# An adaLN feed-forward with threshold routing: x loads first, 17 key levels, layer 1's high parts ahead

## The reference, cut to what matters

```
probs = softmax(rotate(x) @ gate_w.T)                    # N x 8
order = argsort(-probs); csum = cumsum(p_sorted)
select_prefix = experts up to the first with csum >= 0.9
R = p_sorted - rank   (rank 1..8; -1e9 where not selected)
topC = the 512 tokens with the largest R, for each expert
scores = probs where selected and in topC, else 0
y = sum over e of scores[:, e] * (gelu(rotate(x) @ w1[e].T) @ w2[e].T)
out = x + y
```

## Time and profile before

| | us |
|---|---|
| median of three runs | 267.33 |
| the profiled execution's own time | 266.72 |
| its span, first to last instruction | 264.9 |
| TensorE busy with matmuls | 243.7 |
| VectorE busy | 199.4 |
| ACT busy | 149.8 |
| POOL busy | 137.0 |

### The profile page before, as it was taken

The page is one execution under the profiler, slowest core; times in us unless marked ns, Lnnn a source line. Parts: engine busy times, 40 slices in busy tenths (PEclk is TensorE's granted clock), DMA queues, the critical chain, the costliest instruction groups (busy, mean ns, idle before and its releaser), DMA issues.

```text
span 264.9 us, 4043 instructions
## 1 busy us (share of the span) xinstructions
PE 243.7 (92%) x1450; PEld 185.0 (70%) x1450; DVE 199.4 (75%) x430; ACT 149.8 (57%) x275; POOL 137.0 (52%) x105
## 2 busy tenths in 40 slices
PE   7788878798998999999999999999999999999970
PEld 2455433245996888888888888888888888888750
DVE  5288889998989967978996798789779966933220
ACT  6431048864566658746765774687467658734100
POOL 1000000037703987887778749766875771487530
PEclk9999999999999999999999999999999999999997
DMA  6999999407798597579658855973994690372521
GB/s 214 422 424 428 503 343 387 149 21 196 261 317 282 195 344 132 161 179 273 166 82 249 241 111 118 294 192 48 219 249 130 85 222 12 42 85 37 182 91 40
DMA packets 12787, 53.81 MB, mean 203 GB/s; under 512 B 2768, under 2 KB 3152, under 8 KB 9552
## 3 DMA queue, kind: packets, MB, share of 16 engines
q1 hardware_dynamic: 4512, 35.72, 37.2%
q0 software_dynamic: 8256, 17.85, 31.8%
HBM read 44.78 MB, written 18.22 MB: 238 GB/s over the span
## 4 chain that ended last, share of the span: by engine, by line
PE 68%; DVE 16%; DMA 8%; issue 2%; POOL 1%; ACT 1%; SPq 0%; POOLq 0%; DVEq 0%
PE bank L828 21%; PE bank L830 20%; PE bank L829 20%; DMA region<-in_xt 7%; DVE region L691 4%; PE bank L810 4%; DVE w1rot L509 3%; DMA xg<-in_x,gath 1%; PE bank L888 1%; POOL xg L298 1%; DVE hl L538 1%; DVE thr L708 1%; DVE xg L637 0%; DVE xg L633 0%; DVE csum L638 0%
## 5 line engine op out<-in xcount | busy, mean ns | idle before, releaser
L314 POOL DMA_INDIRECT out<-ysb,scat x32 | 61.3, 1916 | 34.8 <-ACT ysb L391 22.2
L509 DVE SCALAR_TENSOR_TENSOR w1rot<-w1raw,rot,w1rot 128x512 f32<-128x512 f32 x84 | 63.1, 751 | 5.3 <-ACT w1rot L351 3.4
L298 POOL DMA_INDIRECT xg<-in_x,gath x16 | 19.8, 1235 | 70.5 <-DVE gath L560 56.3
L828 PE MATMUL bank<-xh,w1h 128*128 128x512 f32 (+1 forms) x144 | 53.2, 370 | 0.1
L830 PE MATMUL bank<-xh,w1l 128*128 128x512 f32 (+1 forms) x144 | 52.7, 366 | 0.0
L829 PE MATMUL bank<-xl,w1h 128*128 128x512 f32 (+1 forms) x144 | 52.7, 366 | 0.0
L828 PE MATMUL bank<-w2h,hh 128*128 128x512 f32 x128 | 51.6, 403 | 0.0
L830 PE MATMUL bank<-w2h,hl 128*128 128x512 f32 x128 | 50.0, 390 | 0.0
L829 PE MATMUL bank<-w2l,hh 128*128 128x512 f32 x128 | 49.9, 390 | 0.0
L538 DVE TENSOR_TENSOR hl<-hf,hh 128x512 fp32r<-128x512 f32 x32 | 22.1, 689 | 28.3 <-ACT hh L382 28.3
L378 ACT ACTIVATE hf<-bank 128x512 f32<-128x512 f32 x32 | 19.1, 597 | 36.1 <-PE bank L830 36.1
(11 more groups left out here) (134 smaller groups left out, 332.7 us busy)
## 6 DMA issues: line engine op xcount, KB each, us to landing
region<-in_xt SPq DMA_DIRECT2D x8, 1024.0 KB, 9.4
w1raw<-in_w SPq DMA_DIRECT2D x8, 1024.0 KB, 12.0
w2raw<-in_w SPq DMA_DIRECT2D x8, 1024.0 KB, 8.6
score<-probs_scratch,pidx POOLq DMA_INDIRECT x32, 5.1
out<-ysb,scat POOLq DMA_INDIRECT x32, 6.0
probs_scratch<-probs SPq DMA_DIRECT2D x1, 384.0 KB, 21.1
ch<-in_ch SPq DMA_DIRECT2D x1, 320.5 KB, 10.2
xg<-in_x,gath POOLq DMA_INDIRECT x16, 4.0
```

Of the source, the lines that this page charges most:

```text
L298: pool.indirect_dma_start(xg[e % 2][:, s, :], None, x_d, bass.IndirectOffsetOnAxis(gath[:, e, s:s + 1], 0)).then_inc(xg_in[e % 2][s], 16)
L314: pool.indirect_dma_start(out_d, bass.IndirectOffsetOnAxis(scat[:, e, s:s + 1], 0), ysb[:, s, :], None, compute_op=ALU.add if e < LAST els ...
L509: ins = nc.vector.scalar_tensor_tensor(dst, w1raw[:, e % 2, i, :], rot[:, j, i:i + 1], dst, ALU.mult, ALU.add)
L828: nc.tensor.matmul(dst, ah, bh, start=first, stop=False)
```

## The change

- SP no longer issues `small` and `cf`; ACT does, as its first two instructions, on its own queue. x blocks 0 and 1 are then SP's first.
- There are 17 levels in place of 23. Above 1.25 the intervals are 0.25 wide, below it 0.125. `scale` (minus 1 or minus 2, by `top`) multiplies the keys, so that the search runs on one width; it is one new instruction of VectorE ahead of the keys and two new ones in round 0. The last two steps of the search use it.
- `gath` is written from the first sum directly, without the minimum; x in HBM has 128 more rows of zeros, which a list that is short can point at. `tabf` is computed after it.
- The first `count_tokens` reads the thresholds from PSUM, and the copy to `tb` comes after its scan.
- `layer1` and `layer1_half` issue high x high and low x high for all four chunks of x, and then the four products with `xl`. They wait for `xh` first and for `xl` later.
- For expert 0, `layer2` tile 1 comes ahead of the second pair of transposes.
- 12 filler matmuls at the start in place of 13.

```
@@ -55,21 +55,18 @@
 THRESHOLD = 0.9
-KEY_ULP = 2.0 ** -24
+KEY_ULP = 2.0 ** -23
 ABOVE = 2.0 ** -24 * (1 + 2.0 ** -20)
...
 G8, G9 = 2.0 ** -8, 2.0 ** -9
-WIDTH = 0.125
+WIDTH, WIDTH1 = 0.25, 0.125
 BINS = ([(0.0, 0.0 - G9)] + [(31 * k * G8, 31 * k * G8 - G9) for k in range(1, 8)]
-        + [(1.25, 1.5 - G9)] + [(k * G8, k * G8 - G9) for k in (415, 446, 477)]
-        + [(2.25, 682 * G8)] + [(k * G8, k * G8 - G9) for k in (714, 745)]
-        + [(3.375, 3.75 - G9), (991 * G8, 991 * G8 - G9)]
-        + [(4.375, 1228 * G8), (1259 * G8, 1258 * G8)]
-        + [(5.375, 1493 * G8), (1524 * G8, 1523 * G8)]
-        + [(6.375, 1755 * G8), (7.375, 2015 * G8), (8.5, 8.5 - WIDTH)])
+        + [(1.25, 1.5 - G9), (447 * G8, 447 * G8 - G9), (2.25, 682 * G8), (745 * G8, 745 * G8 - G9), (3.375, 3.75 - G9),
+           (4.375, 1228 * G8), (5.375, 1493 * G8), (6.375, 1755 * G8), (7.375, 2015 * G8), (8.5, 8.5 - WIDTH)])
 TL = len(BINS) - 1
+SPLIT = 1.25
 NL = TL * E
@@ -83,7 +80,7 @@
 CG, NCG = table(("sel", E), ("slot", S4), ("start", KT), ("need", KT), ("step", ROUNDS * KT), ("offset", ROUNDS * KT),
-                ("last", 1), ("tops", NL))
+                ("tops", NL))
 CA, NCA = table(("same", P), ("ones", P), ("levels", NL))
@@ -154,6 +151,7 @@
         edge = sb("edge", [P, 2])
+        scale = sb("scale", [P, 3])
         tb = sb("tb", [P, E])
@@ -240,8 +238,6 @@
         def _(sp):
-            sp.dma_start(small[:, :], small_d).then_inc(small_in, 16)
-
             def load_x(g):
@@ -259,7 +255,6 @@
-            sp.dma_start(cf[:, :], cf_d).then_inc(cf_in, 16)
             load_x(0)
@@ -340,6 +335,8 @@
         def _(act):
+            act.dma_start(small[:, :], small_d).then_inc(small_in, 16)
+            act.dma_start(cf[:, :], cf_d).then_inc(cf_in, 16)
             act.wait_ge(squares, 1)
@@ -556,20 +553,20 @@
                 then(nc.vector.tensor_reduce(tabg[:, :], before_slot[:, :, :], AX.X, ALU.add))
+                nc.vector.tensor_tensor(gath[:, e, :], tabg[:, :], vbank[:, :, NT], ALU.add).then_inc(gath_ready, 1)
                 then(nc.vector.tensor_tensor(tabf[:, :], tabg[:, :], vbank[:, :, NT], ALU.add))
-                nc.vector.tensor_scalar(gath[:, e, :], tabf[:, :], float(N - 1), None, ALU.min).then_inc(gath_ready, 1)
                 then(nc.vector.tensor_scalar(tabg[:, :], tabf[:, :], float(N - 1), None, ALU.min))
...
-            def count_tokens(e0, e1):
+            def count_tokens(e0, e1, edges=tb):
...
                     ins = nc.vector.tensor_tensor(mask[:, e0:e1, m, :], key[:, :, e0:e1].rearrange("p t e -> p e t"),
-                                                  tb[:, e0:e1].unsqueeze(2).to_broadcast([P, w, NT]), op)
+                                                  edges[:, e0:e1].unsqueeze(2).to_broadcast([P, w, NT]), op)
                 then(ins)
@@ -678,7 +675,8 @@
             dve.wait_ge(key_mm, 1)
-            nc.vector.tensor_scalar(keys[:, :], kbank[:, 0:N // TC], top[:, 0:1], -1.0, ALU.subtract,
+            then(nc.vector.tensor_scalar(scale[:, 0:1], top[:, :], SPLIT, -2.0, ALU.is_ge, ALU.add))
+            nc.vector.tensor_scalar(keys[:, :], kbank[:, 0:N // TC], top[:, 0:1], scale[:, 0:1], ALU.subtract,
                                     ALU.mult).then_inc(thr_ready, 1)
@@ -691,7 +689,11 @@
                 last.then_inc(cnt_v, 1)
-                if r >= 1:
+                if r == 0:
+
+                    nc.vector.tensor_scalar(scale[:, 1:2], scale[:, 0:1], 3.0, -0.5, ALU.add, ALU.mult)
+                    nc.vector.tensor_scalar(scale[:, 2:3], scale[:, 0:1], 3.0, -0.5 * KEY_ULP, ALU.add, ALU.mult)
+                else:
@@ -700,7 +702,7 @@
-                    nc.vector.tensor_scalar(edge[:, 0:1], base[:, now, 0:1], -1.0, top[:, 0:1], ALU.mult, ALU.add)
+                    nc.vector.tensor_scalar(edge[:, 0:1], base[:, now, 0:1], scale[:, 1:2], top[:, 0:1], ALU.mult, ALU.add)
                 dve.wait_ge(cnt_mm, r + 1)
@@ -709,15 +711,15 @@
                 else:
-                    nc.vector.scalar_tensor_tensor(edge[:, 1:2], cgv("last"), best[:, :], edge[:, 0:1],
+                    nc.vector.scalar_tensor_tensor(edge[:, 1:2], scale[:, 2:3], best[:, :], edge[:, 0:1],
                                                    ALU.mult, ALU.add).then_inc(base_ready, 1)
...
             dve.wait_ge(tb_mm, 1)
-            then(nc.vector.tensor_copy(tb[:, :], kbank[:, 0:E]))
             dve.wait_ge(ch_in, 16)
-            count_tokens(0, 2)
+            count_tokens(0, 2, kbank)
+            nc.vector.tensor_copy(tb[:, :], kbank[:, 0:E])
             nc.vector.tensor_copy(rows[:, :, :, NT], chv("rowbase").unsqueeze(1).to_broadcast([P, E, 2])).then_inc(rows_ready, 1)
@@ -836,29 +838,38 @@
                 fs = slice(f * P, (f + 1) * P)
+                dst = hbank[n % 2][:, :]
                 for j in range(C4):
-                    if f == 0 and e >= 1:
+                    if f == 0:
+                        pe.wait_ge(x_hi, C4 * e + j + 1)
+                    nc.tensor.matmul(dst, w1h[e % 2][:, j, fs], xh[:, j, :], start=(j == 0), stop=False)
+                    nc.tensor.matmul(dst, w1l[e % 2][:, j, fs], xh[:, j, :], start=False, stop=False)
+                for j in range(C4):
+                    if f == 0:
                         pe.wait_ge(x_lo, C4 * e + j + 1)
-                    last = split_product(hbank[n % 2][:, :], w1h[e % 2][:, j, fs], w1l[e % 2][:, j, fs],
-                                         xh[:, j, :], xl[:, j, :], j == 0, j == C4 - 1)
+                    last = nc.tensor.matmul(dst, w1h[e % 2][:, j, fs], xl[:, j, :], start=False, stop=(j == C4 - 1))
                 last.then_inc(h_mm, 1)
...
                     pe.wait_ge(w1_lo, C4)
-                    pe.wait_ge(x_lo, S4 // 2)
-                if n == 2:
-                    pe.wait_ge(x_lo, S4)
+                if n % 2 == 0:
+                    pe.wait_ge(x_hi, S4 // 2 * (1 + n // 2))
                 if n >= 2:
...
                     fs = slice(f * P, (f + 1) * P)
+                    dst = hbank[n % 2][:, i * HALF:(i + 1) * HALF]
                     for j in range(C4):
-                        last = split_product(hbank[n % 2][:, i * HALF:(i + 1) * HALF], w1h[0][:, j, fs], w1l[0][:, j, fs],
-                                             xh[:, j, ns], xl[:, j, ns], j == 0, j == C4 - 1)
+                        nc.tensor.matmul(dst, w1h[0][:, j, fs], xh[:, j, ns], start=(j == 0), stop=False)
+                        nc.tensor.matmul(dst, w1l[0][:, j, fs], xh[:, j, ns], start=False, stop=False)
+                    if n % 2 == 0 and i == 0:
+                        pe.wait_ge(x_lo, S4 // 2 * (1 + n // 2))
+                    for j in range(C4):
+                        last = nc.tensor.matmul(dst, w1h[0][:, j, fs], xl[:, j, ns], start=False, stop=(j == C4 - 1))
                 last.then_inc(h_mm, 1)
@@ -927,7 +938,7 @@
             pe.wait_ge(blank_ready, 1)
-            keep_clock(13, kbank, blank)
+            keep_clock(12, kbank, blank)
             pe.wait_ge(gate_folded, 1)
@@ -1023,9 +1034,11 @@
                 layer2(e, 0)
+                if e == 0:
+                    layer2(e, 1)
                 if e + 1 < E:
                     transpose_x(e + 1, (2, 3))
-                for s in range(1, S4):
+                for s in range(2 if e == 0 else 1, S4):
                     layer2(e, s)
@@ -1044,14 +1057,14 @@
     sign = np.where(act, -1.0, 1.0)
-    tops = np.array([o + WIDTH for _, o in BINS])
-    cg[:, slice(*CG["start"])] = -tops[0] * sign
+    lead = WIDTH1 - G9
+    tops = np.array([o + WIDTH1 - lead if at < SPLIT else o + WIDTH - 2 * lead for at, o in BINS])
+    cg[:, slice(*CG["start"])] = -2 * lead * sign
     cg[:, slice(*CG["need"])] = np.where(act, 2.0 * CAP - N, CAP)
...
         cg[:, CG["offset"][0] + r * KT:CG["offset"][0] + (r + 1) * KT] = sign * ((k + 1) * step - act * KEY_ULP / 2)
-    cg[:, CG["last"][0]] = -KEY_ULP
     cg[:, slice(*CG["tops"])] = np.repeat(np.diff(tops), E)[None] * (np.arange(NL)[None] % E == p[:, None] % E)
@@ -1075,9 +1088,9 @@
-    rows = np.ascontiguousarray(np.asarray(x).reshape(N, D))
-
-    xt = np.ascontiguousarray(rows.reshape(P, NG, TPG, C4, P).transpose(1, 4, 3, 2, 0)).reshape(NG, P, C4, TG)
+    rows = np.concatenate([np.asarray(x).reshape(N, D), np.zeros((P, D), np.float32)])
+
+    xt = np.ascontiguousarray(rows[0:N].reshape(P, NG, TPG, C4, P).transpose(1, 4, 3, 2, 0)).reshape(NG, P, C4, TG)
     cond, right = np.asarray(cond_256).T, np.asarray(L0_cond_q_right).T
```

## The result

The changed kernel takes 271.25 us (median of 4 runs, 269.95 to 274.12), the kernel before 267.3: a ratio of 1.0134, 95% interval [1.0083, 1.0186]. It is slower, by 1.3%, and 264.8 was forecast.

What follows compares the result with a forecast made beforehand. TensorE's dense part from 84 us was taken as fixed, the serial path ahead of it as what could shorten. Gains of 0.57 + 0.16 + 0.38 + 1.10 = 2.21 us gave 264.5 to 265.1, put at 264.8; range 263.3 to 266.5.

Steps and rivals of the forecast that it cites:

- the term for `cf`: At the start: `cf`, issued beside x blocks, lands 1.2 us later (bounds 0 and 2.0), gate weights ready at 7.31.
- Rival B: At the start: `cf` waits for x blocks 0 and 1, landing at 8.6; slower, 268.9 us; chance 0.05.
- A: Rival at the start: `cf` waits for all of x block 0 (or ACT's table load); 266.5 us (266.1); chance 0.14.
- x first: At the start: two issues leave SP's queue ahead of x, so the x stream moves 0.75 us earlier.
- 17 levels and scaled keys: VectorE's key chain and search: shorter comparisons and counts less new instructions, a gain of 0.16 us after the first two chunks.
- Row list: Ahead of the first gather: one synchronised instruction and the threshold copy leave the path, 0.19 us each, 0.38 together.
- High parts first: Expert 0's first product no longer waits for low parts; 0 to 0.13 us to be had, counted as 0.
- Tile 1 ahead of the second transposes: Expert 0's output: tile 1 fills TensorE's wait at 81.67; gain 1.10 us, with a new 0.28 wait for tile 0's read-out.
- rival C: At expert 0's output: tile 0's read-out comes 1.1 us later, so the reordering gives nothing; 265.9 us; chance 0.08.
- The sum: Whole kernel: 0.57 (start to chunk 2) + 0.16 (levels, keys) + 0.38 (row list) + 1.10 (tile 1) = 2.21 us gained.

Runs made afterwards that it cites:

- e1: The changed kernel with both small loads (`small`, `cf`) at the head of SP's queue again, ahead of x; 265.45 us, ratio 0.9957.
- e2: The kernel before with only x first on SP and the two small loads on ACT's queue; 273.15 us, ratio 1.0244.
- e4: The changed kernel, small loads still on ACT's queue, with SP waiting for `cf` to land before it issues x; 266.83 us, ratio 1.0015.
- g1: The changed kernel unaltered, measured and profiled again in a later session; 276.03 us, ratio 1.01.
- g4: The changed kernel with 34 filler matmuls at the start instead of 12, in g1's session; 275.01 us, ratio 0.9989.
- f1: e1 with the old 23 levels and plain keys, in a later session; 270.31 us, ratio 0.9836.
- e3: e1 with the sign tables moved from `cf` into `small`, SP issuing small, x0, `cf`, x1; 266.09 us, ratio 0.9978.
- g2: e1 again, in a later session beside g1; 270.42 us, ratio 0.9887.
- f4: e1 with the copies into the output waiting for the gathers of expert 0 instead of expert 1; 272.0 us, ratio 0.991.

## Why the prediction was wrong

**The step that failed is the term for `cf`:** "Bounds 0 and 2.0; I take 1.2." It measured 5.5: `cf` landed at 8.78 instead of 3.27 and facA started 5.49 later; e1, e2 and e4 each show it as the cause, and e2 has it alone. The price came from a gather of 256 KB beside 1 MB loads, the nearest row. That row has the other order: its two loads had been issued at 71.39 and 71.95, 12 us ahead of the gather at 83.50. At the start, x0 and x1, 2 MB, stood beside `cf` from the same instant on. What that row could not give was an upper bound, and I used it as one.

**Rival B was true, and had 0.05.** It put `cf` at 8.6 (measured 8.78), the gate weights at 11.4 (11.60) and a time of 268.9. Of the 2.35 us from there to 271.25 B left out one part that is shown: TensorE fell to its lower level in the wait, which g1 and g4 price at 1.0 to 1.9. B had the second gate product at 13.6; it started at 15.55, and with the clock kept up (g4) at 14.06. Chunk 2 came at 28.81 instead of B's 26.2 (26.69 in g4).

The landings have a pattern that B had and A had not. The x loads of the changed kernel (L244), the first by itself, and the first two:

```profile
DMA to landing us min/median/max: 5.1/5.1/5.1
...
DMA to landing us min/median/max: 5.1/6.3/7.4
```

`small`, issued with x0, landed at 6.04, where x0 landed at 0.74 + 5.1 = 5.84; `cf`, issued with x1 at 1.18, landed at 8.78, where x1 landed at 1.18 + 7.4 = 8.58. Each small load landed 0.2 us behind the block it was issued with. In e2 it is the same: x0 at 6.24 and `small` at 6.44, x1 at 8.97 and `cf` at 9.17. The Trainium skill, "DMA: Bandwidth & Descriptors", section "Queues, rings and completion order", says that an engine takes some 9 to 17 descriptors from one row's ring before it turns to the next; the prediction worked out 6.0 to 8.5 for `cf` by it. The trace nearly agrees: 8.78 stands just above that range. I had the rule, its number and a measured row beside each other, and gave the row the weight though it measured something else. Its rule on completion increments is no less consistent with these rows, and no run here tells the two apart.

**x first, the rest of it:** the x loads were issued 0.89 earlier, and the first two landed 1.0 and 0.7 earlier, where 0.75 was forecast; ACT's table load did follow the issues (1.66). Neither mattered, as x no longer was what the gate waited for. In e1, where x is as before, VectorE still waits 0.49 us at chunk 2 for TensorE's logits. So the stream is a bound there; that x first would be worth something if `cf` weren't needed follows from it, but no run shows it.

**17 levels and scaled keys:** 0.20 for each chunk was forecast, 0.21 measured; the counts 0.16 for 0.10; the new instruction 0.19 with its wait for 0.24; the keys themselves 0.54 instead of 0.48, 0.06 that was not forecast. Behind chunk 2 the whole of it gained 0.30 (f1 against e1) for 0.16.

**Row list:** 0.39 measured (f1), 0.38 forecast. With the two instructions of round 0 and the longer keys, keys to gather is 0.28 shorter in the changed kernel; 0.38 less 0.10 was forecast.

**High parts first:** nothing was forecast, and no run tried it by itself. Expert 0's first product follows the first gather after 6.77 (e1) to 7.09 us (e3) in the first session's profiles and after 7.23 before, but e2, which has the old products, has 7.07.

**Tile 1 ahead of the second transposes, 1.10:** the mechanism was right, and so was the size as long as POOL's gathers came on time: 1.26 and 0.85 us in e3 and e4, with a wait for the read-out of none and 0.32 where 0.28 was forecast. What failed was the premise that the read-out comes as it did before. In the changed kernel's profile and in e1's (the slowest of its 10 runs) the wait at the transposes went, and the wait for the read-out took its place with 1.92 and 2.14 us, with the lower clock behind it. That is rival C's mechanism, which had 0.08; but what made the copies late is not the change. e1:

```profile
66.11 2.83 POOL L296 DMA_INDIRECT region<-in_x,gath  x1 [0.30 <-issue]
...
84.74 0.69 ACT L389 ACTIVATE ysb<-bank,score 128x512 f32<-128x512 f32 x1 [4.25 <-DMA score<-probs_scratch,pidx]
85.48 0.79 PE L831 MATMUL bank<-w2h,hh 128*128 128x512 f32 x1 [2.14 <-ACT ysb L389]
```

In both profiles one gather issue of POOL ahead of the copies took 2.83 us instead of 0.95, and the copies, which wait for the gathers, came 1.9 later. In the kernel before, e3, e4, g1 and g2 a score issue took 1.89, which the copies do not wait for, and of these the four with the new order have at most 0.32 us of wait for the read-out of tile 0. g1 and g2 are the changed kernel and e1 once more, so the slow issue goes with the execution and not with the kernel. That e1's runs of 264.6 to 265.1 are those without a slow gather issue fits this, but it was only argued: in that session only one execution of e1 was profiled.

**The sum** of the parts other than the loads was forecast at 1.64 us. e1 gains 1.16 against its session's median and g2 4.15, so the forecast lies between. Why g2 gains more isn't settled; its start and first gather were no earlier than e1's.

## What to carry to other kernels

A small load that the first computation needs belongs ahead of the large ones: issued beside them, even on another queue and at the same instant, it landed when they did. Here it cost them 0.9 us ahead of them, and itself 5.5 beside them. A price read from a row holds as a bound only if order and sizes are the same, so before a load with no slack is moved, write down what is in flight when it is issued, and let a rule that speaks against the move set the upper end of the range. Where a wait stands ahead of matmuls, add to its price that TensorE's clock may have fallen behind it. And where a step takes up another engine's slack, look at how much that engine's own times vary: a late one costs more than the step gains.

## What had not been expected of the hardware

- `small` (38.5 KB) took 1.7 to 1.9 us ahead of the x loads, on either queue, and 5.3 to 5.7 beside the first 1 MB block; `cf` (80 KB) 1.9 to 2.7, and 7.6 to 8.0 beside two.
- After 5 us of idle TensorE a gate product took 1.93 instead of 1.08 us at a granted 0.50; after 2.54 us of idle in e4 it took 1.94 too, after 1.95 in g2 1.68, and after 1.52 in g4 and 0.30 in e1 1.08 and 1.09.
- In 17 of the 18 profiles one of POOL's first twelve indirect DMA issues takes 1.9 or 2.83 us instead of 0.95: in 13 of them the ninth, the first for scores, with 1.9, in the changed kernel, e1, e2 and f4 the eighth, the last gather of expert 1, with 2.83. It isn't the kernel that decides, as g1 and g2 show. What does is open.
- In the later sessions, where the kernel before took 7.1 to 8.4 us more, ACT stood for 3.3 to 7.6 us at its first activation of the first layer in every profile but f4's, and TensorE had waits that the profile puts down to nothing but the issue. In g2 the matmuls that this activation reads had ended by 67.7 us. g2, ACT and TensorE:

```profile
72.16 0.60 ACT L376 ACTIVATE hf<-bank 128x512 f32<-128x512 f32 x1 [6.04 <-remote]
...
72.11 0.28 PE L869 MATMUL bank<-xh,w1l 128*128 128x256 f32 x1 [0.72 <-issue]
```

The first session's e1 has this activation at 66.79 behind 1.67 us of wait for TensorE. From expert 0's first product to its tile 0 it is 13.1 us in every profile of the first session and 16.9 to 18.8 in the later ones. The profile names no releaser in the kernel, and the kernel before wasn't profiled in those sessions, so this cause stays open.
